# A transformer block pair on one core: gate logits taken from the attention's own products, rows stored before they are normalised

## The reference

```
x += tanh(g_xattn[0]) * softmax((LN(x) Wq + bq)(ctx Wk + bk)^T) (ctx Wv + bv)       # one head
x += tanh(g_ffn[0])   * moe(LN(x))      # logits = LN(x) gate_w^T + expert_bias, 12 experts, top 2,
                                        # softmax over the two; 8 experts: w2 silu(w1 x); 4 "zero" experts: x
x += tanh(g_xattn[1]) * attention of 16 heads with 16 columns each, output projection Wo
x += tanh(g_ffn[1])   * linear layer with weight and input quantised to fp8
```

## Time and profile before

| what | us |
|---|---|
| median of three runs | 374.39 |
| lowest, highest | 371.9, 374.43 |
| span of the profiled execution | 378.3 |
| TensorE busy in that span | 348.3 |
| VectorE busy | 261.1 |
| ScalarE busy | 219.8 |
| GpSimd busy | 154.3 |

### The profile page before, as it was taken

One profiled execution on the slowest core, in us unless ns is written; L12 is line 12 of the kernel. 1 busy time (PEld: TensorE's weight loads), 2 busy tenths in 40 slices (PEclk: granted clock), 3 DMA queues, 4 the chain that ended last, 5 costly groups with the idle time before them and its releaser, 6 DMA issues.

```text
span 378.3 us, 9027 instructions
## 1 busy us (share of the span) xinstructions
PE 348.3 (92%) x2959; PEld 279.9 (74%) x2960; DVE 261.1 (69%) x659; ACT 219.8 (58%) x452; POOL 154.3 (41%) x197
## 2 busy tenths in 40 slices
PE   3997889988999999999999998879999999998995
PEld 2776769756799999999999994556676667666674
DVE  2588984685646556654554447888789888957696
ACT  2589856742444544554454452456767787774586
POOL 6279967204355556555555535412130331101100
PEclk9999975598999999999999999999999999999999
DMA  6999902221133333322322213410110100000005
GB/s 180 327 413 419 419 30 83 86 84 49 50 99 111 125 108 102 123 83 71 81 69 76 76 40 114 154 57 2 57 58 11 50 2 2 2 5 0 2 28 196
DMA packets 15386, 38.25 MB, mean 101 GB/s; under 512 B 3574, under 2 KB 4748, under 8 KB 13820
## 3 DMA queue, kind: packets, MB, share of 16 engines
q1 hardware_dynamic: 10556, 26.74, 19.5%
q0 software_dynamic: 3936, 10.45, 9.4%
q10 hardware_dynamic: 864, 0.66, 0.6%
HBM read 24.34 MB, written 13.50 MB: 100 GB/s over the span
## 4 chain that ended last, share of the span: by engine, by line
PE 77%; DVE 12%; ACT 5%; DMA 3%; issue 2%; POOL 0%; POOLq 0%
PE two L1964 15%; PE two L1977 14%; PE two L2113 5%; PE two L1996 4%; PE two L2143 4%; PE two L2178 4%; PE two L2099 4%; PE two L2079 3%; PE two L1814 2%; PE two L1987 2%; PE two L2170 2%; PE two L1790 1%; DVE negmax L1133 1%; DMA ident<-in_c_ident 1%; PE two L2159 1%
## 5 line engine op out<-in xcount | busy, mean ns | idle before, releaser
L1364 DVE SCALAR_TENSOR_TENSOR gate<-th,two 128x512 f32<-128x512 f32 x39 | 26.8, 688 | 58.3 <-ACT th L842 32.5
L842 ACT ACTIVATE th<-two 128x512 f32<-128x512 f32 x39 | 23.4, 599 | 71.0 <-PE two L1977 52.8
L585 POOL DMA_INDIRECT y_d<-y_sb,goal_i x39 | 38.5, 988 | 50.4 <-ACT y_sb L852 50.4
L579 POOL DMA_INDIRECT xg<-xn_d,slot_i x39 | 38.0, 974 | 32.3 <-DVE slot_i L1315 14.8
L1964 PE MATMUL two<-wh,gh 128*128 x156 | 44.2, 283 | 0.1
L1964 PE MATMUL two<-wh,gl 128*128 x156 | 44.0, 282 | 0.0
L1964 PE MATMUL two<-wl,gh 128*128 x156 | 43.8, 281 | 0.0
L599 POOL TENSOR_TENSOR rstd<-var,half 128x2 f32<-128x2 f32 x14 | 9.9, 708 | 76.7 <-DVE var L1431 76.7
L1464 DVE TENSOR_REDUCE nm<-two 128x8 f32<-128x960 f32 x32 | 36.1, 1152 | 4.5 <-PE two L2099 4.1
L544 POOL TENSOR_TENSOR wl<-wl,wh 128x512 fp32r<-128x512 f32 x26 | 34.2, 1337 | 8.1 <-ACT wh L726 8.1
L1977 PE MATMUL two<-wh,xh 128*128 x78 | 34.2, 438 | 1.4 <-DVE xl L1358 1.4
(11 more groups left out here) (298 smaller groups left out, 883.3 us busy)
## 6 DMA issues: line engine op xcount, KB each, us to landing
wl<-in_wmoe SPq DMA_DIRECT2D x8, 1024.0 KB, 14.2
y_d<-wh SPq DMA_DIRECT2D x4, 1024.0 KB
yg<-y_d SPq DMA_DIRECT2D x7, 512.0 KB, 3.4
xn_d<-xq SPq DMA_DIRECT2D x8, 256.0 KB, 2.0
xz<-xn_d SPq DMA_DIRECT2D x8, 256.0 KB
out_x<-of SPq DMA_DIRECT2D x8, 256.0 KB, 2.0
x_sb<-in_x SPq DMA_DIRECT2D x1, 1024.0 KB, 10.1
x_sb<-in_x SPq DMA_DIRECT2D x1, 768.0 KB, 4.7
```

Source lines behind the costliest of these rows:

```text
L579: pool.indirect_dma_start(xg[:, n % 2, :], None, xn_d, bass.IndirectOffsetOnAxis(ap=slot_i[:, n:n + 1], axis=0)).then_inc(gathered[n % 2], 16)
L585: pool.indirect_dma_start(y_d, bass.IndirectOffsetOnAxis(ap=goal_i[:, n:n + 1], axis=0), y_sb[:, n % 2, :], None).then_inc(y_stored[n % 2] ...
L842: nc.scalar.activation(th[:], bank[2 + k][:], ACT.Tanh, scale=0.5).then_inc(th_ok, 1)
L1364: dve.scalar_tensor_tensor(gate[:, k, :], th[:], 1.0, bank[2 + k][:], ALU.add, ALU.mult).then_inc(gate_ok, 1)
```

## The change

- The 12 centred gate columns are written behind the 120 key columns of `kq` once per chunk, so that `scores0` gives 132 columns: scores, and x times gate. They are kept in `xgate` (VectorE). Likewise the values get 12 columns (values times gate), so that `attend` gives the gate's share of the attention's output; `add_x1` adds it to `xgate`. `transpose_x1`, `copy_xT1` and `gate_of` are gone. `logits_of` only multiplies by the inverse deviation; two `bias_logits` add the expert bias.
- The gain is put into the values' weights, the values' bias comes in through a second small product; `copy_v0` is now a plain copy on ScalarE. Four transposes of the values' weights and bias and four small products make the 12 columns once.
- `norm1` and the `xz` path are gone. x has 258 columns per tile in SBUF; the last two hold the inverse deviation and the negative mean times it. SyncE stores these raw rows as soon as `root1` has written the two columns. After the gather VectorE normalises the block (`norm_of`), then TensorE transposes it. The zero experts' part is made in place from x itself with `keep_x` and `add_x`.
- All 32 low parts are on GpSimd, the order of parts is by layer from part 20 on, 10 of them stand behind the last `root1` and ahead of the wait for `slots_kept`, 4 between the first gathers. TensorE waits for 25 low parts before the first products and for all 32 before the first full pair.
- The order of TensorE, ScalarE and VectorE in the first attention is written anew. `weights` is cut in three, each behind a slot of the expert loop.
- x is loaded in eight pieces instead of three.

```diff
+            def values_gate():
+                pe.wait_ge(gate_ok0, 1)
+                pe.wait_ge(wvT_kept, 1)
+                for k in range(2):
+                    for c in range(C):
+                        ins = pe.matmul(bank[3][:, k * E_ALL:(k + 1) * E_ALL], wvT[:, k, c, :],
+                                        kq[:, 0, c * KP + LK:(c + 1) * KP], ...)
...
             def scores0(b):
...
                 for u in range(U):
-                    dst = bank[6 + b % 2][:, u * LK:(u + 1) * LK]
-                    pe.matmul(dst, spread0[:, b % 2, u, :], kq[:, b, cols(C, LK)], start=True, stop=False, ...)
+                    dst = bank[6 + b % 2][:, u * KP:(u + 1) * KP]
                     for c in range(C):
-                        ins = pe.matmul(dst, xT[:, b, c, u, :], kq[:, b, cols(c, LK)], ...)
+                        pe.matmul(dst, xT[:, b, c, u, :], kq[:, b, cols(c, KP)], ...)
+                    ins = pe.matmul(dst[:, 0:LK], spread0[:, b % 2, u, :], kq[:, b, C * KP:C * KP + LK], ...)
...
             def max0_of(b):
...
+                dve.tensor_copy(xgate[:, b], at[:, :, LK:KP])
                 own.settle()
-                dve.tensor_tensor(negmax[:, b % 2, :], lowest[:, b % 2, :], rstd0[:, b, :], ALU.mult).then_inc(max_done, 1)
+                for u in range(U):
+                    ins = dve.tensor_scalar(negmax[:, b % 2, u:u + 1], lowest[:, b % 2, u:u + 1], rstd0[:, b, u:u + 1], None,
+                                            ALU.mult)
+                ins.then_inc(max_done, 1)
...
             def add_x1(b):
...
+                for u in range(U):
+                    dve.scalar_tensor_tensor(xgate[:, b, u, :], at[:, u, D:VP], rsum[:, u:u + 1], xgate[:, b, u, :], ALU.mult,
+                                             ALU.add)
...
             def logits_of(b):
-                dve.wait_ge(logit_done, b + 1)
                 dve.wait_ge(rstd1_ok, root_of(b, ROOTS1))
                 for u in range(U):
+                    ins = dve.tensor_scalar(logit[:, cols(2 * b + u, E_ALL)], xgate[:, b, u, :], x_rstd(2 * b + u), None, ALU.mult)
                 ins.then_inc(logit_kept, 1)
+            def bias_logits(lo, hi):
+                dve.wait_ge(gate_in, 32)
+                dve.wait_ge(logit_kept, hi)
+                at = logit[:, lo * U * E_ALL:hi * U * E_ALL].rearrange("p (t e) -> p t e", e=E_ALL)
+                dve.tensor_tensor(at, at, gbias_sb[:, 0:E_ALL]. ... , ALU.add).then_inc(biased, 1)
...
+        FIRST_LAYER = [j for j in range(20, CHUNKS) if j % 4 < 2]
+        SECOND_LAYER = [j for j in range(20, CHUNKS) if j % 4 > 1]
+        HIGHS = list(range(20)) + FIRST_LAYER + SECOND_LAYER
+        LOWS = list(range(19)) + FIRST_LAYER + [19] + SECOND_LAYER
...
+            root1(6)
             low(17)
+            root1(7)
+            lows(18, 28)
             pool.wait_ge(slots_kept, 1)
             def gather(n):
-                wait(pool, xgT_done, n - 1)
+                wait(pool, xq_ok, n - 1)
...
-            for n in range(AHEAD):
-                gather(n)
+            gather(0)
+            gather(1)
+            lows(28, 30)
+            gather(2)
+            gather(3)
+            low(30)
+            gather(4)
+            low(31)
+            gather(5)
...
+            def norm_of(i, k):
+                wait(dve, gathered[k], 16 * (i + 1))
+                wait(dve, xgT_done, 2 * i + k - 1)
+                dve.tensor_scalar(xq[:, k, :], xg[:, k, 0:D], xg[:, k, D:D + 1], xg[:, k, D + 1:D + 2], ALU.mult,
+                                  ALU.add).then_inc(xq_ok, 1)
...
             def slot(i, k):
                 if live(i, k, 4):
                     xl_of(*ahead_of(i, k, 4))
+                if live(i, k, 5):
+                    norm_of(*ahead_of(i, k, 5))
...
-            pe.wait_ge(split_l, CHUNKS - len(VECTOR_LOW))
-            pe.wait_ge(split_d, len(VECTOR_LOW))
+            pe.wait_ge(split_l, LOWS.index(FIRST_LAYER[-1]) + 1)
...
+            pe.wait_ge(split_l, CHUNKS)
             pair(0)
```

More of the change, by code:

```diff
@@ L28 @@
 TILES = B * U
+XP = D + 2
+KP = LK + 12
+VP = D + 12
 C = D // P
@@ L45 @@
 NB = 4
-NX = 4
 HG = HEADS // NB
@@ L345, in build @@
             "of_ok")
+        x_in = [sem(f"x_in{k}") for k in range(4)]
         chunk_in = [sem(f"chunk_in{k}") for k in range(LOADS)]
@@ L540, in low, with lows @@
-            def low(j):
-                pool.wait_ge(split_h, j + 1)
-                c = cols(j, CHUNK)
+                pool.tensor_tensor(less, less1[:].rearrange("p b u -> p (b u)")[:, t], rstd, ALU.mult).then_inc(rstd1_ok, 1)
+            def low(n):
+                pool.wait_ge(split_h, HIGHS.index(LOWS[n]) + 1)
+                c = cols(LOWS[n], CHUNK)
                 pool.tensor_tensor(wl[:, c], wl[:, c].bitcast(F32), wh[:, c], ALU.subtract).then_inc(split_l, 1)
+            def lows(lo, hi):
+                for n in range(lo, hi):
+                    low(n)
@@ L546, in _ @@
             root0(0)
             root0(1)
-            for j in range(0, 5):
-                low(j)
+            lows(0, 3)
             root0(2)
+            lows(3, 5)
+            root0(3)
             low(5)
-            for j in range(7, 10):
-                low(j)
-            for j in range(11, 14):
-                low(j)
-            for j in range(15, 17):
-                low(j)
-            root1(0)
-            low(17)
-            for j in range(19, 22):
-                low(j)
@@ L562, in _ @@
-            for j in range(23, 25):
-                low(j)
-            root1(1)
-            low(25)
-            low(27)
-            root1(2)
-            for j in range(28, 30):
-                low(j)
-            root1(3)
-            low(30)
-            root1(4)
-            low(31)
+            root1(0)
+            lows(6, 8)
+            root1(1)
+            lows(8, 10)
+            root1(2)
+            lows(10, 12)
+            root1(3)
+            lows(12, 14)
+            root1(4)
@@ L791, in _ @@
[L791 to L807 removed]
+            copy_v0(1)
+            copy_xT(3)
+            high(3)
+            copy_v0(2)
@@ new lines, in _ @@
+            spread_std(3)
+            copy_keys(4)
+            copy_probT(1)
+            high(4)
+            exp0_of(2)
+            high(5)
+            copy_keys(5)
+            spread_std(4)
+            copy_xT(4)
+            highs(6, 8)
+            exp0_of(3)
+            copy_probT(2)
+            spread_std(5)
+            high(8)
+            copy_v0(3)
+            copy_xT(5)
+            high(9)
+            exp0_of(4)
+            copy_probT(3)
+            high(10)
+            copy_v0(4)
@@ new lines, in _ @@
+            spread_std(6)
+            copy_xT(6)
+            high(11)
+            exp0_of(5)
+            copy_probT(4)
+            high(12)
+            copy_v0(5)
+            spread_std(7)
+            copy_xT(7)
+            high(13)
+            exp0_of(6)
+            copy_probT(5)
+            copy_v0(6)
+            highs(14, 16)
+            copy_v0(7)
+            exp0_of(7)
+            copy_probT(6)
+            high(16)
+            copy_probT(7)
+            highs(17, CHUNKS)
@@ L1873, in _ @@
+            transpose_x0(4)
+            transpose_prob(2)
+            values0(3)
+            attend(2)
+            scores0(4)
+            transpose_x0(5)
+            transpose_prob(3)
+            values0(4)
+            attend(3)
+            scores0(5)
             transpose_x0(6)
+            transpose_prob(4)
             values0(5)
-            transpose_prob(2)
-            scores0(4)
-            transpose_x1(0)
-            attend(2)
+            attend(4)
+            scores0(6)
```

562 lines of the change are left out of this document (241 added, 321 removed).

## The result

The changed kernel takes 391.38 us (median of 4 runs, 386.5 to 392.76) where the kernel before, on the same chip, takes 374.41 (4 runs, 371.9 to 377.45). A second measurement, 4 runs against 13 of the kernel before, gave 388.2 us and 1.040 (1.030 to 1.050). The forecast was 374 us in a range of 365 to 379, with 0.26 for slower. It was wrong.

A forecast was written before the change was run, and what follows sets the result against it. The expert loop, bound by TensorE, starts after `slot_i`, behind attention and VectorE's routing chain; `slot_i` 0.4 us earlier and first blocks +0.3 gave -0.1 on a 378.3 us span, hence 374 us, range 365 to 379.

The forecast's parts named there:

- Last logits at 62.7 us: End of first attention: VectorE gets its last logits at 62.7 us, 10.3 earlier than 73.03.
- attend(2), forecast near 36: First attention: walking the first three batches through the later durations puts attend(2) near 36 us, attend(5) near 51.2.
- rival 3: Attention, attend(5) to attend(7): TensorE's clock falls as before, +4.2 us, or +8 from the third batch; 378 us; chance 0.26.
- The cycle itself, 5.1 us: First attention: the queues go round once per batch through TensorE and ScalarE, 5.1 us a batch with hand-overs.
- 10.3 earlier than 73.03: Gain up to the last logits, counted from the profiled kernel before, whose last logit came at 73.03 us.
- Carrying that difference over: Whole time: the profiled span, 378.3 us, lies 3.9 above the runs' median of 374.39; that difference was kept.
- The routing is 9.9 us longer: Routing: ten dependent two-input VectorE instructions each wait for a GpSimd low part; 9.9 us, between 0 and 12.7.
- Rival 1: Routing: the lock bites less; without it `slot_i` is at 76.5 us and the time 364.5, half of it 369; chance 0.24.
- The first blocks: +0.3: Between `slot_i` and the first expert blocks: normalisation, later gathers and moved `weights` sum to +0.3 us, between -1.5 and +1.5.
- -1.9 for the moved `weights`: First blocks: eight `weights` instructions leave the spot before the third block's xl, where TensorE waited: -1.9 us.
- The loop itself: 0: Expert loop and all behind it: no change, 0 us, with 3.5 us per block held fixed.
- The two-port rule: Attention: tensor_scalar may also exclude GpSimd, so logits wait for low parts; up to 1 us a batch, time 378.

The follow-up runs named there:

- the run with all low parts early: Changed kernel with GpSimd's last four low parts moved from between the gathers to behind the ten after the last root, nothing left out: 388.75 us.
- the repeat: The kernel before, executed and profiled once more with no edit: 372.0 us, one run.

## Why the prediction was wrong, step by step

Against the profile of the kernel before, the forecast was -10.3 until the last logit, +9.9 in the routing and +0.3 in the first blocks. The trace has -2.1, +8.4, +2.6 and +0.9 in the loop: 9.9 us of span.

**"Last logits at 62.7 us" failed, by 8.3 us, and is the step that decided.** Three pieces, measured against its own walk. attend(2), forecast near 36, starts at 40.35 (+4.4): the first scores come at 22.37 us, 5 us later than in the kernel before, of which 3.2 are the half speed of this execution's start (19.22 in the run with all low parts early, which has attend(2) at 37.79), and then ScalarE's queue puts 2.7 us of other work between the transposes of prob(2) and their copy. I took the cycle from the later batches and applied it where the queues of the first batches have two high parts and a spread in it. From attend(2) to attend(5) the forecast has 15.2 us and the trace 18.0, since one step of 7.8 fell under the low clock (part of rival 3, in an earlier place). From attend(5) to the last logit 11.5 and 12.6. The cycle itself, 5.1 us, is right to a hundredth, and so is its path through ScalarE: leaving out all low parts did not change it, and ScalarE's order did. By the run with the full clock, whose last logit came at 66.56, some 4.4 of the 8.3 us were half speed of this execution and 3.9 the walk's own error.

**The same step compared with the wrong point.** It called the shift "10.3 earlier than 73.03". Of those, 8.4 us were the low clock of one execution, which the repeat does not show (64.58). Measured against that, even a last logit at 62.7 was worth 2 us. Counted from the repeat (span 370.2, `slot_i` kept at 78.1), the same steps give +8.6 us, some 380.6 us of time as an estimate, since a time lies some 1.8 us above its span in every run here. That would have been slower, and still some 8 us short. What the row could have told: the runs of before spread over 2.5 us already in the three times shown, and the profiled span lay 3.9 us above their median. With the 1.8 us the profiled execution took some 380.1 us, 5.7 above the median, and its mean clock of 0.964 is that of the longest runs (380.4 and 380.8). Carrying that difference over as a constant hid it: it belonged to one term.

**"The routing is 9.9 us longer" was right in its mechanism, and 1.5 us too much.** From the last logit to `rows_up` 14.7 us for a forecast of 16.2, to `slot_i` 22.0; +8.4 over before. Ten instructions met ten low parts, but not the ten that were named: they were the two logits, the bias, and eq to hot; pairs and dif ran free, since the low parts had ended at 83.84. Two experiments show it from both sides: -7.6 us from the last logit to `slot_i` when the ten are left out, +6.9 when they are put into the kernel before. Rival 1 is out.

**"The first blocks: +0.3" failed.** It was +2.6 (repeats +3.0), outside its bounds of -1.5 to +1.5. I counted the four low parts between the gathers as a delay of gather 2 only, not as a lock on the norm that the change had just put on VectorE: two norms took 2.12 us and one 0.84, for 0.40 each. Leaving the four out gives 3.5 us back: 1.4 of these waits, and 2.1 of TensorE's clock on the first products, a term that the sum did not have. Against the repeat of the kernel before, the first product comes 0.3 us later after `slot_i` without low parts (5.8 for 5.5), and the first y 0.8 us sooner after that product (10.1 for 10.9), where the forecast had -1.9 for the moved `weights`.

**"The loop itself: 0" was off by 0.9.** Its 38 steps take 127.8 us for 126.9. In the steps behind the moved `weights` instructions one y follows another after up to 4.03 us for 3.5; one later step takes 3.99. No experiment separated these, so that `weights` is the cause is argued, not shown.

**The two-port rule.** The new logits and norms are tensor_scalar instructions that read SBUF, and they waited as the others did: 1.18 us for two logits beside one low part, 2.44 beside two, 2.12 for two norms. So the trace agrees with what the Trainium skill says in SBUF — State Buffer, section Who interferes with whom: tensor_scalar can enter a mode that takes the ports shared with GpSimd. No run here separates that mode from the factors per partition that the instructions also read from SBUF; `negmax` reads one too and did not wait (below). The price that I gave it, up to 1 us a batch in attention, did not arise: without low parts the attends stood at the same times. It was paid once at the last logit (2.1 us) and at the norms (1.4).

**Where the rivals stood.** Rival 3, slower by the clock, had the sign. It placed the low clock at attend(5) to attend(7), or for longer from the third batch on; the low clock did cost 1.7 to 2.7 us after attend(2), for one step alone, and 2.1 on the first expert products, which no rival had. None had the larger mechanism, that the gain I subtracted was not there. The attention of the change is worth 3 to 4 us (last logit at 60.53 without low parts and 61.71 with all of them, for 64.58), but only with ScalarE's queue, and GpSimd's where it has low parts, in another order.

## What to carry to other kernels

Before a stall of the profile is booked as a gain, ask whether a second execution would show it: a spread of the runs as large as the stall says it may not. When work moves between queues, walk the first batches apart from the steady cycle, and ask of every small wait on another engine (here a root of 0.7 us) what stands ahead of it in that engine's queue. And here a bulk job on GpSimd cost VectorE's dependent chain 0.7 to 0.8 us per piece of 1.27 us (6.9 and 7.6 for ten, 3.0 for four), on whichever side of the wait it stood. Where such a wait also lets TensorE stand idle, look at the clock behind it before the whole loss is put down to the lock.

## What the runs showed that I had not expected

- One program, executed again, had TensorE's granted clock at 0.50 from 52 to 73 us once and at 1.00 the other time; the last logit moved by 8.4 us. Its runs spread over 371.5 to 380.8 us.
- The granted clock read 1.00 for the first 20 us of an execution whose matmuls took twice as long as in another until 19.4 us (1.95 us for 1.05); their durations show it.
- tensor_scalar on single columns (`negmax`, 128x1) did not wait beside a low part (two in 0.33 us at 34.70, under GpSimd's low part of 34.41, all low parts early), while two of 12 columns (1.2 to 2.4 us for 0.36) and one of 256 columns (0.84 for 0.40) did.
- An edit that is worth -7 us without GpSimd's low parts (376.1 to 369.1) was worth +9 with them (388.2 to 397.1): in a ring of queues that run in order, an improvement of one engine can set the whole pace.
